# Score maxima from stacks of their own, with 512 columns in each matmul, in a reordered slot

## The reference

```python
scores = jnp.einsum('bhqd,bhkd->bhqk', q, k) / math.sqrt(HD)
scores = scores + mask[None]            # causal: -inf above the diagonal; ALiBi: slope_h * (k - q)
attn = jax.nn.softmax(scores, axis=-1)
out = jnp.einsum('bhqk,bhkd->bhqd', attn, v)
...
x = x + (h @ ffn2_w[i].T + ffn2_b[i])
```

## Time and profile before

| what | us |
|---|---|
| median of 3 runs | 1738.49 |
| lowest, highest | 1737.05, 1749.57 |
| profiled execution | 1739.33 |
| its span | 1737.2 |

### The profile page before, as it was taken

The page is one execution under the profiler, slowest core; times in us unless marked ns, Lnnn a source line. Parts: engine busy times, 40 slices in busy tenths (PEclk is TensorE's granted clock), DMA queues, the critical chain, the costliest instruction groups (busy, mean ns, idle before and its releaser), DMA issues.

```text
span 1737.2 us, 41352 instructions
## 1 busy us (share of the span) xinstructions
PE 1495.2 (86%) x12256; PEld 1123.2 (65%) x12256; DVE 1128.3 (65%) x3106; ACT 1204.7 (69%) x2165; POOL 608.8 (35%) x1051
## 2 busy tenths in 40 slices
PE   0777777499999989999999899999998999899995
PEld 0445554267777767777777677777776766677663
DVE  6566775356666656677666666666675666677662
ACT  3233333168888878788888787888887877778774
POOL 5223331223333333333333333333333344444433
PEclk9999999689999999999999999999999999999998
DMA  4333332232222222322222223222222232222210
GB/s 114 98 92 110 102 98 61 74 91 75 75 73 73 73 79 73 90 73 82 82 70 78 77 74 90 78 82 78 73 73 79 74 93 79 73 80 80 79 50 10
DMA packets 99910, 137.24 MB, mean 79 GB/s; under 512 B 15809, under 2 KB 81985, under 8 KB 99841
## 3 DMA queue, kind: packets, MB, share of 16 engines
q1 hardware_dynamic: 85024, 100.07, 20.2%
q0 software_dynamic: 14848, 36.74, 7.2%
HBM read 70.54 MB, written 65.01 MB: 78 GB/s over the span
## 4 chain that ended last, share of the span: by engine, by line
PE 60%; DMA 14%; issue 8%; DVE 6%; ACT 4%; SPq 4%; POOL 1%; DVEq 0%; POOLq 0%; ACTq 0%
PE mxp L870 13%; PE exp_ps L897 11%; PE pvp L920 10%; DMA qbd_l<-split_L 8%; PE mxp L876 6%; PE dense L818 4%; PE dense L846 4%; PE dense L959 3%; DMA qbd_l<-negt 3%; PE dense L950 3%; ACT exp_ps L805 2%; DVE negm L648 2%; PE dense L938 2%; PE dense L853 2%; DMA qbd_f<-split_F 1%
## 5 line engine op out<-in xcount | busy, mean ns | idle before, releaser
L784 ACT ACTIVATE probs<-exp_ps 128x512 f32<-128x512 f32 x896 | 525.2, 592 | 396.3 <-PE exp_ps L897 395.5
L648 DVE TENSOR_REDUCE negm<-mxp 128x2 f32<-128x512 f32 (+1 forms) x1152 | 609.5, 567 | 152.5 <-PE mxp L876 119.6
L870 PE MATMUL mxp<-kst_l,qbd_l 127*128 127x256 f32 x2048 | 402.2, 307 | 32.0 <-DMA qbd_l<-split_L 27.1
L897 PE MATMUL exp_ps<-qbd_l,kst_l 128*128 128x512 f32 x768 | 365.4, 490 | 63.1 <-ACT exp_ps L805 48.3
L870 PEld LDWEIGHTS mxp<-kst_l,qbd_l 127*128 127x128 f32 x2048 | 356.8, 196 | 69.6 <-DMA qbd_l<-split_L 26.8
L805 ACT ACTIVATE exp_ps<-masktf 128x512 f32<-128x512 f32 x513 | 308.4, 601 | 16.7 <-DVE rest L716 6.4
L876 PE MATMUL mxp<-maskb,identb 128*128 128x256 bf16 x1024 | 294.1, 287 | 0.0
L458 POOL TENSOR_SCALAR veps<-mv 128x2 f32<-128x2 f32 x144 | 31.9, 222 | 658.5 <-DVE mv L606 655.2
L920 PE MATMUL pvp<-probs,vst_l 128*32 128x256 f32 (+1 forms) x4096 | 219.5, 332 | 0.1
L897 PEld LDWEIGHTS exp_ps<-qbd_l,kst_l 128*128 128x128 f32 x768 | 144.3, 195 | 115.5 <-ACT exp_ps L805 57.7
L694 DVE COPY ost<-pvp 128x512 f32<-128x512 f32 x80 | 55.3, 692 | 209.6 <-PE pvp L920 209.6
(11 more groups left out here) (93 smaller groups left out, 1984.5 us busy)
## 6 DMA issues: line engine op xcount, KB each, us to landing
split_L<-hi SPq DMA_DIRECT2D x256, 128.0 KB, 2.1
kst_l<-split_L SPq DMA_DIRECT2D x64, 384.0 KB
split_L<-lo POOLq DMA_DIRECT2D x128, 128.0 KB, 2.1
qbd_l<-split_L SPq DMA_DIRECT2D x128, 96.0 KB
qbd_l<-split_L POOLq DMA_DIRECT2D x128, 96.0 KB, 3.0
split_F<-hi SPq DMA_DIRECT2D x64, 128.0 KB, 2.1
kst_f<-split_F SPq DMA_DIRECT2D x16, 384.0 KB, 4.1
split_F<-lo POOLq DMA_DIRECT2D x32, 128.0 KB, 2.3
```

The lines of the kernel that those rows point to most:

```text
L648: dve.tensor_reduce(negm[:, s, qt, h0:h0 + 2], mxp[:, (plan.max_chunks * g + ch) % 3, :].rearrange("p (h t) -> p h t", h=2)[:, :, 0:keys], ...
L784: act.activation(probs[:, g[0], ch, :], exp_ps[:, (plan.exp_chunks * g[0] + ch) % 2, :], ACT.Exp, scale=plan.scale).then_inc(q.b_exp, 1)
L870: last = pe.matmul(mxp[:, bank, k * T:(k + 1) * T], qbd[plan.name][0:MAX_ROW, s, h, qt * P:(qt + 1) * P], kst[plan.name][0:MAX_ROW, s, g[0 ...
L897: pe.matmul(exp_ps[:, bank, :], kst[plan.name][:, s, g[0], kt * P:(kt + 1) * P], rhs, start=not on_diagonal, stop=True, skip_group_check=T ...
```

## The change

For the encoder the maxima no longer use `kst` and `qbd`. They get two tiles of their own. `qst` holds the queries of the four heads of a group in 96 rows, and is stationary. `kbd` holds the keys of each head in its own 24 rows, with zeros elsewhere, and moves. One matmul then makes 512 columns: for the first 128 queries four heads with 128 keys each, for the second 128 queries two heads with 256 keys each. A unit has 12 chunks in place of 16, each with one matmul in place of two; the mask matmul of the first kind has 512 columns. Each reduction reads 512 elements. `kbd` shares its memory with `qbd` of the first part, so that GpSimd clears it between the parts, and four small transfers put the bias rows in.

Both new tiles are single-buffered. Their load is the new step `stack_max+`: SP issues 384 KB for `qst` and two transfers of 96 KB for `kbd`, GpSimd two more of 96 KB, once the parts of that unit are written and the last maximum of the unit before is computed. The old load, `stack+`, now all on SP (one transfer of 384 KB and four of 96 KB), comes one slot later, behind `op`.

The order of the slot changes too: 12 chunks are spread from `exp` 2 to `exp` 9, the first two groups of `pv` come behind `exp` 8 and the last two behind `f1`, and `stack_max+` stands ahead of `negt+`. A seed follows directly behind the exponential that empties its bank. `at` moves to bank 0 of `dense`, `f2` to bank 1.

```diff
-        self.max_chunks = NT * self.hg // 2
+        self.max_chunks = 3 if causal else 2
         self.exp_chunks = 3 if causal else 2
         self.slot = 16 if causal else 32
-        self.stack_dmas = self.hg // 2 + 1
-        self.pool_stack_dmas = self.hg // 2
+        self.stack_dmas = self.hg + 1 if causal else self.hg // 2 + 1
+        self.max_dmas, self.pool_dmas = self.hg // 2 + 1, self.hg // 2
         self.units = 2 * rounds
+        self.at_bank = 0 if causal else 1
+
+    def max_bank(self, ch):
+
+        if not self.causal:
+            return ch, 0, 2
+        return (0, 0, 4) if ch == 0 else (1, 2 * (ch - 1), 2)
 
     def slot_steps(self, s, last_layer):
 
@@ -70,38 +78,34 @@
...
-        maxes = [("max", s + 1, g, ch) for g in range(GROUPS) for ch in range(self.max_chunks)]
-        first_exps = [("exp", s, 0, 0), ("exp", s, 0, 1)]
-        out = at("ot", s - 1) + at("ln", s + 2) + at("ot+", s - 1) + at("xn", s + 2)
-
-        out = first_exps + out if self.causal else out + first_exps
-        out += at("f2 f2+", s - 2) if ff else []
-        out += at("at at+", s - 1)
-
-        first_max, more = (2, 2) if self.causal else (4, 1)
-
-        after = [
-            at("v v+", s + 1) + at("xt", s + 2),
...
+        exps = [("exp", s, *divmod(k, self.exp_chunks)) for k in range(self.exp_chunks * GROUPS)]
+        maxes = [("max", s + 1, *divmod(k, self.max_chunks)) for k in range(self.max_chunks * GROUPS)]
+        values = [("pv", s, g) for g in range(GROUPS)]
+
+        if self.causal:
+            end, end2, store = (at(k, s - 2) if last_layer else [] for k in ("end", "end+", "store"))
+            return (
+                exps[0:2] + at("ot", s - 1) + at("ln", s + 2) + at("ot+", s - 1) + at("v v+", s + 1) + at("xn", s + 2)
+                + at("f2 f2+", s - 2) + at("at at+", s - 1)
+                + exps[2:3] + maxes[0:1] + at("xt", s + 2)
+                + exps[3:4] + maxes[1:3] + at("xt+", s + 2) + at("op", s - 1) + at("stack+", s + 1)
+                + exps[4:5] + maxes[3:4] + at("op+", s - 1) + at("qk", s + 2)
+                + exps[5:6] + maxes[4:6] + at("qk+", s + 2)
+                + exps[6:7] + maxes[6:7] + end
+                + exps[7:8] + maxes[7:9] + at("xn2", s - 1)
+                + exps[8:9] + maxes[9:10] + values[0:2] + at("xt2", s - 1)
+                + exps[9:10] + maxes[10:12] + at("xt2+", s - 1) + end2 + at("stack_max+", s + 2)
+                + exps[10:11] + at("negt negt+", s + 1)
+                + exps[11:12] + at("f1 f1+", s - 1) + values[2:4] + at("pv+", s) + store)
...
+        blocks = sb("blocks", [P, 2 * EXPERT.heads, T], F32R)
+        qbd = {"L": sb("qbd_l", [P, 2, ENCODER.heads, T], F32R),
+               "F": blocks.rearrange("p (s h) t -> p s h t", s=2)}
+        kbd = blocks.rearrange("p (g i) t -> p g i t", g=GROUPS)
+        qst = sb("qst", [P, GROUPS, T], F32R)
...
+            def stack_for_maxima(plan, q, u, r, s):
+                sc, rows = split[plan.name][s], COPIES * plan.dh
+                parts_written(q, r, s)
+                wait_past(sp, q.b_max, plan.max_chunks * GROUPS * u)
+                settle(sp, passed_sp)
+                sp.dma_start(qst[0:plan.hg * rows, :, :].bitcast(F32),
+                             sc[0].rearrange("i c d (g t) -> (i c d) g t", t=T)).then_inc(q.max_stk[s], 16)
+                for i in range(plan.hg // 2):
+                    sp.dma_start(kbd[i * rows:(i + 1) * rows, :, i, :].bitcast(F32),
+                                 sc[1, i].rearrange("c d (g t) -> (c d) g t", t=T)).then_inc(q.max_stk[s], 16)
+
+            def stack_queries_and_keys(plan, q, u, r, s):
+                sc, rows = split[plan.name][s], COPIES * plan.dh
+                parts_written(q, r, s)
                 wait_past(sp, q.b_s, plan.exp_chunks * GROUPS * (u - 1))
                 settle(sp, passed_sp)
-                rows = COPIES * plan.dh
                 sp.dma_start(kst[plan.name][0:plan.hg * rows, s, :, :].bitcast(F32),
                              sc[1].rearrange("i c d (g t) -> (i c d) g t", t=T)).then_inc(q.stk[s], 16)
                 qd = qbd[plan.name][:, s].bitcast(F32).rearrange("p (g i) t -> p g i t", g=GROUPS)
-                for i in range(plan.hg // 2):
+                for i in range(plan.hg if plan.causal else plan.hg // 2):
                     sp.dma_start(qd[i * rows:(i + 1) * rows, :, i, :],
                                  sc[0, i].rearrange("c d (g t) -> (c d) g t", t=T)).then_inc(q.stk[s], 16)
 
             def share(plan, q, step, u, s, r):
...
+            sp.wait_ge(s_cleared, 1)
+            sp.wait_ge(s_rounded, 6)
+            for i in range(ENCODER.hg):
+                rows = slice(ALIBI_ROW + 2 * i, ALIBI_ROW + 2 * i + 2)
+                sp.dma_start(kbd[rows, :, i, :].bitcast(F32), kst["L"][rows, 0, :, :].bitcast(F32)).then_inc(s_bias, 16)
...
+            pool.memset(blocks[0:ALIBI_ROW].bitcast(F32), 0.0).then_inc(s_cleared, 1)
+            pool.wait_ge(s_cleared, 1)
...
-                        if plan.causal and ch > 0:
-                            act.wait_ge(q.b_exp, plan.exp_chunks * G + ch)
-                            seed((plan.exp_chunks * g[0] + ch - 1) % 2)
                         act.wait_ge(q.b_s, plan.exp_chunks * G + ch + 1)
                         act.activation(probs[:, g[0], ch, :], exp_ps[:, (plan.exp_chunks * g[0] + ch) % 2, :], ACT.Exp,
                                        scale=plan.scale).then_inc(q.b_exp, 1)
+                        if plan.causal and ch < 2:
+                            act.wait_ge(q.b_exp, plan.exp_chunks * G + ch + 1)
+                            seed((plan.exp_chunks * g[0] + ch) % 2)
...
-                        qt, pair = ch % NT, ch // NT
-                        for k in range(2):
-                            h = plan.hg * g[0] + 2 * pair + k
-                            last = pe.matmul(mxp[:, bank, k * T:(k + 1) * T],
-                                             qbd[plan.name][0:MAX_ROW, s, h, qt * P:(qt + 1) * P],
-                                             kst[plan.name][0:MAX_ROW, s, g[0], :],
-                                             start=(k == 0), stop=True, skip_group_check=True)
+                        qt, first, count = plan.max_bank(ch)
                         if plan.causal:
-                            o = mxp[:, bank, :].rearrange("p (h t) -> p h t", h=2)[:, :, qt * P:(qt + 1) * P]
-                            last = pe.matmul(o, identb[:, :], maskb[:, :, :], start=False, stop=True,
+                            keys = 512 // count
+                            pe.matmul(mxp[:, bank, :], qst[0:BIAS_END, g[0], qt * P:(qt + 1) * P],
+                                      kbd[0:BIAS_END, g[0], first:first + count, 0:keys], start=True, stop=True,
+                                      skip_group_check=True)
+                            o = mxp[:, bank, :].rearrange("p (h t) -> p h t", h=count)[:, :, qt * P:(qt + 1) * P]
+                            last = pe.matmul(o, identb[:, :], maskb[:, 0:count, :], start=False, stop=True,
                                              skip_group_check=True)
+                        else:
+                            for k in range(count):
+                                last = pe.matmul(mxp[:, bank, k * T:(k + 1) * T],
+                                                 qbd["F"][0:MAX_ROW, s, plan.hg * g[0] + k, qt * P:(qt + 1) * P],
+                                                 kst["F"][0:MAX_ROW, s, g[0], :],
+                                                 start=(k == 0), stop=True, skip_group_check=True)
                         last.then_inc(q.b_max, 1)
                     elif step == "negt":
...
-                        dense_job(0, q.c_done, 1, off + BATCH)
+                        dense_job(1, q.c_done, 1, off + BATCH)
```

More of the change, by code:

```diff
@@ L95, in slot_steps @@
-        for k in range(2, 3 * GROUPS):
-            g, ch = divmod(k, 3)
-            if ch < self.exp_chunks:
-                out.append(("exp", s, g, ch))
-            if k >= first_max:
-                out += maxes[more * (k - first_max):more * (k - first_max + 1)]
-            out += after[k - 2]
-        out += at("f1 f1+", s - 1) if ff else []
-        out += [("pv", s, GROUPS - 1)] + at("pv+", s) + at("stack+", s + 2)
-        return out + (at("store", s - 2) if last_layer else [])
+        exps = [("exp", s, *divmod(k, self.exp_chunks)) for k in range(self.exp_chunks * GROUPS)]
@@ L175, in __init__ @@
         self.stk = [sem(f"{name}_stk{s}") for s in range(2)]
+        self.max_stk = [sem(f"{name}_max_stk{s}") for s in range(2)]
         self.pool_stk = [sem(f"{name}_pool_stk{s}") for s in range(2)]
@@ L502, in steps @@
                             pool.dma_start(dst, lo[:, s, qk * T:(qk + 1) * T].bitcast(F32)).then_inc(q.lo_parts[s], 16)
-                    elif step == "stack+":
+                    elif step == ("stack_max+" if plan.causal else "stack+"):
```

(10 more changed lines are left out.)

91 lines of the change are left out of this document (56 added, 35 removed).

## The result

The changed kernel takes 1904.99 us (median of 4 runs, 1897.12 to 1913.55) against 1738.92: a ratio of 1.094, 95% interval 1.087 to 1.101. It is slower by 166 us. I had forecast slower, 1788 us, with a range up to 1835. The direction holds, and so does the chain that I made responsible: SP's load, the transfer of the maxima, the first `exp`. Two of its terms were too small. The maxima land later than I made it, because of transfers on GpSimd's queue that I had weighed too lightly, and SP comes to its load later, because TensorE's clock falls.

The account below looks back on a forecast made before the run. Two chains of nearly one length, TensorE's work and `negt`, transfer, `exp`, were taken to set the slot. Regular slots +38, last layer +6, start +5 and 1 more: together +50 on 1739.3, thus 1788 us; range 1700 to 1835.

Parts of the forecast that it names:

- the chain that I made responsible: Regular slot: SP's load, then the maxima's transfer at T + 18.0 (T: slot's first `exp`), landing 3.4 us later: 21.4 us.
- TensorE saves 1.1 us a slot, and its slot would be 19.7 us: TensorE, regular slot: fewer matmul and mask columns save 1.1 us; with stall and waits counted, 20.5 becomes 19.7 us.
- The wait of 0.8 us ahead of `negt`: TensorE: `negt` waits nearly 1 us for the last two chunks' reductions, an `exp` covering 0.23; taken as 0.8 us.
- SP comes to the load at T + 15.9, set by the landing of the parts: SP, from the slot's first `exp` (T): waits for unit s + 2's parts until T + 15.9, bounds 15.7 and 16.2.
- The maxima land in 3.4 us, at most 3.9: The 16 KB transfer behind SP's 576 KB, GpSimd sending 192 KB more: issue to landing 3.4 us, bounds 2.9 and 3.9.
- the 2.9 that I took for a landing with nothing ahead: The maxima's transfer: lower bound of its landing, 2.9 us as in the kernel before, as if nothing stood ahead.
- A regular slot: + 0.9, at 21.4 us: About 42 regular slots: 21.4 us against 20.5, 0.9 longer each, bounds 0.2 and 1.7; +38 us in all.
- The last layer: - 0.5 to + 1.3, taken + 0.4: Some 16 last-layer slots: 0.66 us of waiting goes, the same chain stands in; +0.4 us each against 21.92, +6 in all.
- The start of the encoder: + 5: Encoder start: GpSimd's clearing and four small transfers put TensorE's first work at 317.0 against 311.94 us, +5.
- the gain comes through: Rival: maxima issued by T + 16.6 (T: slot's first `exp`), landing in 2.9 us; TensorE's 19.7 us slot, 1702 us; chance 0.25.
- costlier matmuls: Rival: each of 12 new matmul chunks takes 0.2 us more than 0.23; slot 22.1 us, about 1838 us; chance 0.05.
- my upper bound: The maxima's landing if they can't be through before SP's load: 5.96 us behind its first issue, 3.9 behind their own.

Follow-up runs that it names:

- the two filled versions: The changed kernel with ten or five added float32 matmuls of 256 columns behind each encoder unit's last `pv`: 1921.46 us with ten, 1828.95 us with five.
- the first experiment: The changed kernel with `stack_max+` moved behind `negt+`, so SP sends the maxima ahead of `qst` and `kbd`: 1687.2 us, 0.969 of the kernel before.
- the old order: The kernel before, old stacks and matmuls, with the encoder's `stack+` loaded ahead of SP's transfer of the maxima: 1946.33 us, one run, against 1732.13.

## Why the prediction was right in kind and wrong in size

- **TensorE saves 1.1 us a slot, and its slot would be 19.7 us.** Right. Most slots are 19.7 to 19.8 us where the maxima don't bind.
- **The wait of 0.8 us ahead of `negt`.** Right: 0.86.
- **SP comes to the load at T + 15.9, set by the landing of the parts.** Right at full clock, T + 15.6 and 15.8 in the two filled versions. Wrong in the changed kernel, T + 17.2, outside the bounds. This is the first failed step. I let TensorE wait 1.7 us at the first `exp` and counted the work behind the wait at the durations of the kernel before. The wait became one of 2.2 us and more, and in 46 of 47 slots the granted clock is at half in it or right behind it. The work from the first `exp` to `qk` then takes 1.4 us more, and it lies ahead of the parts, of the load and so of the next maxima. The slow start does not use up the wait, since what ends the wait is put back by as much: the clock falls again in the next slot. Filling the wait gave back 76 us.
- **The maxima land in 3.4 us, at most 3.9.** The second failed step, and the root of the first: where the maxima land no later than forecast, in the version with GpSimd's transfers behind them and in the last layer, the waits are mostly under 2 us and the clock holds in 44 of 53 slots and in all of the last eleven that wait. The median landing is 4.3 in the slots that count, the longest 5.4. I weighed SP's 576 KB, which alone give 2.7 to 3.0, and let GpSimd's 192 KB pass in half a sentence; they make the difference. The trace of the kernel before had a sign of it: in a regular slot GpSimd's two transfers leave 0.15 us ahead of the maxima (1041.83), in the last layer 1.1 us behind them (1667.64):

```profile
1041.68 1.21 POOL L513 DMA_DIRECT2D qbd_l<-split_L  x2 [2.65 <-PE exp_ps L897]
...
1668.78 1.29 POOL L513 DMA_DIRECT2D qbd_l<-split_L  x2
```

  The maxima landed in 2.9 us there and in 2.2 here (medians). So the 2.9 that I took for a landing with nothing ahead was one with these 192 KB ahead. The bound also came from a load with nothing behind it. I had called `stack+` behind the maxima covered, since nothing waits for it soon; it costs them 0.4 us in the median.
- **A regular slot: + 0.9, at 21.4 us.** It is + 3.2 on average. In the slot shown 1.3 us more until the load and 0.9 more of landing turn the 21.4 into 23.6. Where GpSimd's transfers go behind the maxima, the step holds: 20.6 us in the slot shown of that version, 21.8 on average, + 0.5 over the kernel before. So some 30 us of the loss are what the forecast's mechanism costs (1763.71 against 1734.09 beside it), where I had + 50, and 141 what the two transfers add, with the clock behind the longer wait.
- **The last layer: - 0.5 to + 1.3, taken + 0.4.** Within the bounds: 21.5 against 21.8, - 0.3, with its slots at 21.0 to 21.3 for the most part. Its waits are 1.2 to 1.8 us, and two `exp` behind them take 0.72.
- **The start of the encoder: + 5.** Right, 5.25 (317.19 against 311.94):

```profile
317.19 0.66 PE L862 MATMUL dense<-ident,xn 128*128 128x128 f32 x2 [9.27 <-DMA blocks<-kst_l]
```

- **The rivals.** That the gain comes through with the maxima ahead of the load is what the first experiment shows; in the changed kernel it could not. No sign of costlier matmuls.

The rule of the Trainium skill (DMA: Bandwidth & Descriptors, section Queues, rings and completion order) on the order within a ring, beside my upper bound, pointed to a late landing. But the ring is not the reason: from ScalarE's ring the transfer was as late, and behind the same 576 KB of its own ring it was not late once GpSimd's transfers were gone.

## What to carry to other kernels

A small transfer that the next stage waits for must stand ahead of large ones that nobody needs soon, on every queue and also when those are ready first: look at what all queues have in flight at its issue, the other engines' too, not only at its own queue. When a change is costed and leaves a new wait on TensorE of some two microseconds or more, cost the work behind it at the lower clock, and ask whether that work leads round to the same wait. Where a kernel has a part in which the same chain runs at another speed, as the last layer here, compare the queues of the two parts first: the cause stood there in one trace.

## What the runs showed of the hardware

- A pair of float32r matmuls of 256 columns takes 0.24 us, one of 512 columns 0.23 to 0.24: only columns count, and fewer instructions with the same columns would bring nothing here.
- How long a transfer of 16 KB takes to land, by what was issued ahead of it (medians): 2.2 us with nothing ahead and GpSimd's 192 KB 0.2 us or more behind; 2.7 to 2.9 with only GpSimd's 192 KB, 0.1 to 0.15 us ahead; 2.7 to 3.0 with SP's 576 KB 2.1 us ahead and GpSimd's behind; 3.7 with SP's 384 KB 0.6 and GpSimd's 0.1 us ahead; 4.2 to 4.3 with SP's 576 KB 2.1 and GpSimd's 1.5 us ahead and 768 KB soon behind (3.8 with those 768 KB later, 3.7 in the old order); 4.5 with SP's 0.7 and GpSimd's 0.1 us ahead. From SP's or ScalarE's queue it is the same. That SP's load is mostly gone 2.1 us behind its issue would fit all of them; it is argued, not shown.
- TensorE's clock has two levels in these traces, full speed (2.4 GHz) and half (1.2 GHz). In the changed kernel it was at half for a while around the first `exp` in 46 of 47 slots, where that `exp` waited 2.2 us or more for the maxima. In the last layer, behind eleven waits of 1.2 to 1.8 us, it stayed whole. In the version with GpSimd's transfers behind the maxima it fell in nine of 53 slots, all with waits of 1.8 us or more; between 1.8 and 2.2 us both are seen. The first matmuls behind a wait can still be at full speed, as at 548.85, and the work some 1.5 us behind them at half, so that they alone don't tell whether the clock fell.
- With 2.4 us of filling work ahead of that `exp` the clock fell around it in one of 40 slots that still wait (3.3 us in that one), and adding work made the kernel 4% faster.
